# Attention values on 64 stationary columns in alternate column halves, with row sums made elementwise, in an fp32 language-model tower

## The reference, cut to what matters

```python
q = _l2norm(q) * q_scale
k = _l2norm(k) * k_scale
sim = jnp.einsum('bhid,bhjd->bhij', q, k) * SCALE
sim = sim + slopes * bias
sim = jnp.where(causal[None, None], -neg, sim)
attn = jax.nn.softmax(sim, axis=-1)
out = jnp.einsum('bhij,bhjd->bhid', attn, v)
return out.transpose(0, 2, 1, 3).reshape(b, n, h * dh) @ Wout
```

## Time and profile before

| | |
|---|---|
| median of 3 runs | 3293.55 us (3285.09 to 3293.67) |
| profiled execution | 3293.74 us, span from first to last instruction 3291.9 us |
| mean granted TensorE clock | 0.989 of full speed |
| busy: PE, PEld | 3111.8 us (95%), 1854.0 us (56%) |
| busy: DVE, ACT, POOL | 1701.1 us (52%), 1347.8 us (41%), 606.2 us (18%) |
| instructions | 42125 |

### The profile page before, as it was taken

How to read it: one execution, slowest core, us unless ns; L and a number is a source line. 1 busy time by engine, 2 the same in 40 slices (tenths; PEclk the granted TensorE clock), 3 DMA queues, 4 the chain that set the end, 5 groups by cost and what they waited for, 6 DMA issues and landing times.

```text
span 3291.9 us, 42125 instructions
## 1 busy us (share of the span) xinstructions
PE 3111.8 (95%) x14465; PEld 1854.0 (56%) x14465; DVE 1701.1 (52%) x4049; ACT 1347.8 (41%) x2588; POOL 606.2 (18%) x1020
## 2 busy tenths in 40 slices
PE   1699999999999998999999999999999999999999
PEld 1365656565555554656565656565555555666666
DVE  4555545454555557555554555454555553444444
ACT  2244544454545454545444545454545443111111
POOL 4430303030323031213030303030303000000000
PEclk9899999999999998999999999999999999999999
DMA  1000000000010000000000000000000100000000
GB/s 33 20 16 6 15 6 17 4 17 4 18 28 20 1 20 1 15 6 15 6 15 6 17 4 17 4 17 4 20 1 16 58 1 0 1 1 26 1 0 26
DMA packets 72100, 41.38 MB, mean 13 GB/s; under 512 B 14929, under 2 KB 70865, under 8 KB 71889
## 3 DMA queue, kind: packets, MB, share of 16 engines
q1 hardware_dynamic: 70352, 34.50, 4.0%
q0 software_dynamic: 1536, 4.20, 0.4%
HBM read 17.55 MB, written 4.19 MB: 7 GB/s over the span
## 4 chain that ended last, share of the span: by engine, by line
PE 89%; DVE 5%; issue 2%; ACT 2%; POOL 2%; DMA 0%; SPq 0%; DVEq 0%; ACTq 0%; POOLq 0%
PE ps L1034 29%; PE ps L994 8%; PE ps L1086 8%; PE ps L1072 7%; PE ps L1018 7%; PE ps L1044 7%; PE ps L1019 7%; PE ps L965 7%; PE ps L962 4%; PE ps L979 2%; PE ps L1022 1%; DVE h L820 1%; ACT arena L618 1%; DVE mx L794 1%; PE ps L996 1%
## 5 line engine op out<-in xcount | busy, mean ns | idle before, releaser
L636 ACT ACTIVATE probs<-ps,btab 128x512 f32<-128x512 f32 (+4 forms) x1408 | 831.3, 591 | 1143.9 <-PE ps L1019 628.6
L794 DVE TENSOR_REDUCE mx<-ps 128x1 f32<-128x512 f32 (+4 forms) x1408 | 794.4, 568 | 921.4 <-PE ps L994 504.0
L1034 PE MATMUL ps<-probs,arena 128*128 128x512 f32 (+4 forms) x2816 | 1234.1, 518 | 0.0
L1034 PEld LDWEIGHTS ps<-probs,arena 128*128 128x128 f32 (+1 forms) x2816 | 478.5, 190 | 125.9 <-ACT probs L636 18.1
L994 PE MATMUL ps<-arena 66*128 66x512 f16 (+4 forms) x1408 | 477.5, 341 | 19.9 <-DVE mx L794 8.8
L1018 PE MATMUL ps<-arena 128*128 128x512 f16 (+4 forms) x1408 | 467.8, 332 | 2.0 <-DMA arena<-augs 2.0
L1019 PE MATMUL ps<-arena 65*128 65x512 f16 (+4 forms) x1408 | 468.5, 333 | 0.0
L1044 PE MATMUL ps<-wo,otf 128*128 128x257 f32 x1024 | 316.0, 390 | 17.9 <-ACT arena L618 16.2
L965 PE MATMUL ps<-wqkv,xT 128*128 128x256 f32 (+1 forms) x1088 | 281.8, 382 | 0.0
L535 POOL TENSOR_TENSOR rnorm<-nsq,minus_half 128x4 f32<-128x4 f32 (+1 forms) x272 | 276.8, 1018 | 22.7 <-POOL nsq L532 0.2
L532 POOL TENSOR_SCALAR nsq<-ssq 128x4 f32<-128x4 f32 (+1 forms) x272 | 61.5, 226 | 1188.2 <-DVE ssq L760 1188.2
(11 more groups left out here) (121 smaller groups left out, 2625.2 us busy)
## 6 DMA issues: line engine op xcount, KB each, us to landing
arena<-arena SPq DMA_DIRECT2D x256, 64.0 KB, 2.1
wqkv<-in_Wkv SPq DMA_DIRECT2D x32, 128.0 KB, 2.4
arena<-in_w SPq DMA_DIRECT2D x2, 2048.0 KB, 11.3
out<-h SPq DMA_DIRECT2D x8, 512.0 KB, 2.9
wqkv<-in_Wq SPq DMA_DIRECT2D x16, 128.0 KB, 2.5
wo<-in_Wout SPq DMA_DIRECT2D x32, 64.0 KB, 2.2
h<-in_table,idx POOLq DMA_INDIRECT x32, 2.8
arena<-augs SPq DMA_DIRECT2D x32, 4.0 KB, 1.7
```

What stands on the lines that cost most here:

```text
L636: nc.scalar.activation(probs[0:rows, n % 4, 0:w], bank(S0 + n % 2)[0:rows, 0:w], ACT.Exp, bias=btab[0:rows, hh, z:z + 1]).then_inc(exp_don ...
L794: nc.vector.tensor_reduce(mx[:, it, c:c + 1], bank(k % 2)[:, 0:w], AX.X, ALU.max).then_inc(a_read, 1)
L1034: mm(bank(O0 + o % 2)[:, c0:GW], vt[t % 2][0:rows, jt, hd:hd + 2, :].rearrange("p a d -> p (a d)"), probs[0:rows, n % 4, 0:GW - c0], start ...
```

## The change

The stationary operand of L1034 becomes the 64 columns of values alone. In the groups ig = 1, 2 and 3 even key tiles go to array columns 0 to 63 (bank partitions 0 to 63) and odd ones to columns 64 to 127 (partitions 64 to 127); in group 0 all go to the first half. Two blocks, an even and the odd `m` behind it, are put at one time of the plan, so that their products follow each other. `probs` has 6 buffers.

The row sums: every block's exponentials are added to a tile `acc` (a copy for jt = 0), by POOL in groups 0 and 3 and by DVE in groups 1 and 2 (`sum_p`). At a group's end one product `sums` of 64 stationary columns of ones with `acc` gives the sums in a shared bank, which ACT copies (`keep_sums`). The two halves of a group's bank are joined: ACT copies the upper half to `otb` (`keep_o`), DVE adds the lower half to it (`join`) into `otf`. `wout` and `add_o` stay what they are, two units later. Some steps have times moved by 0.1 to 0.3 units, and the gate's small tiles move into the arena.

```diff
     def attend(t, t0):
         for m in range(PAIR):
             at(t0 + m, "scores", t, m)
             at(t0 + m + 0.5, "exp", t, m)
-            at(t0 + m + 2.4, "values", t, m)
+            at(t0 + m + 1.6, "sum_p", t, m)
+            at(t0 + (m | 1) + 2.4, "values", t, m)
         for hd in range(2):
             for ig in range(NG):
-                e0 = t0 + hd * BLKS + last_block[ig] + 3.7
-                at(e0, "keep_o", t, hd, ig)
+                e0 = t0 + hd * BLKS + last_block[ig] + 5.7
+                at(e0 - 1.5, "sums", t, hd, ig)
+                at(e0 - 1.0, "keep_o", t, hd, ig)
+                at(e0 - 1.0, "keep_sums", t, hd, ig)
+                at(e0 - 0.4, "join", t, hd, ig)
                 for k in range(G):
                     at(e0 + 0.8 + 1.6 * k, "wout", t, hd, ig, k)
-                    at(e0 + 1.5 + 1.6 * k, "add_o", t, hd, ig, k)
+                    at(e0 + 1.4 + 1.6 * k, "add_o", t, hd, ig, k)
...
+    def side(ig, jt):
+        return jt % 2 if ig else 0
...
+                if jt == 0:
+                    need(pool, l_ready, o - 1)
+                    pool.tensor_copy(a, probs[0:rows, n % PB, 0:GW - c0]).then_inc(sum_pool, 1)
+                else:
+                    pool.tensor_tensor(a, a, probs[0:rows, n % PB, 0:GW - c0], ALU.add).then_inc(sum_pool, 1)
...
             def exp(t, m):
-                need(act, pv_done, n - 3)
+                need(act, pv_done, n - PB + 1)
+                if n >= PB:
+                    on_pool, count = summed[n - PB]
+                    act.wait_ge(sum_pool if on_pool else sum_dve, count)
...
             def keep_o(t, hd, ig):
-                nc.scalar.activation(otf[:, o % 2, :], bank(O0 + o % 2), ACT.Copy).then_inc(o_read, 1)
+                if ig:
+                    need(act, joined, joins[o] - 1)
+                    nc.scalar.activation(otb[:, :], bank(O0 + o % 2)[DH:128, :], ACT.Copy).then_inc(o_read, 1)
+                else:
+                    nc.scalar.activation(otf[0:DH, o % 2, :], bank(O0 + o % 2)[0:DH, :], ACT.Copy).then_inc(o_read, 1)
...
+            def join(t, hd, ig):
+                    nc.vector.tensor_tensor(otf[0:DH, o % 2, :], bank(O0 + o % 2)[0:DH, :], otb[:, :], ALU.add).then_inc(joined, 1)
...
             def values(t, m):
-                mm(bank(O0 + o % 2)[:, c0:GW], vt[t % 2][0:rows, jt, hd:hd + 2, :].rearrange("p a d -> p (a d)"), probs[0:rows, n % 4, 0:GW - c0],
-                   start=(jt == 0), stop=(jt == G * ig + G)).then_inc(pv_done, 1)
+                z = side(ig, jt)
+                mm(bank(O0 + o % 2)[DH * z:DH * z + DH, c0:GW], vt[t % 2][0:rows, jt, hd, :], probs[0:rows, n % PB, 0:GW - c0],
+                   start=(jt == z), stop=(jt == G * ig + G - z)).then_inc(pv_done, 1)
+
+            def sums(t, hd, ig):
+                pe.wait_ge(sum_pool if on_pool else sum_dve, count)
+                z = shared_bank("sums", t, hd, ig)
+                mm(bank(z)[DH:128, :], ones[:, :], acc[:, o % 2, :], start=True, stop=True).then_inc(l_ready, 1)
```

More of the change, by code:

```diff
@@ L51, in lm_tower_kernel @@
     last_block = [max(m for m in range(BLKS) if blocks[m][0] == ig) for ig in range(NG)]
+    def side(ig, jt):
+        return jt % 2 if ig else 0
+    summed = {}
+    for n in range(PAIRS * 2 * BLKS):
+        on_pool = blocks[n % BLKS][0] in (0, NG - 1)
+        summed[n] = (on_pool, 1 + sum(1 for i in summed if i // (2 * BLKS) == n // (2 * BLKS) and summed[i][0] == on_pool)
+                     + sum(1 for m in range(2 * BLKS) if (blocks[m % BLKS][0] in (0, NG - 1)) == on_pool) * (n // (2 * BLKS)))
+    joins = {}
+    for o in range(PAIRS * 2 * NG):
+        joins[o] = sum(1 for i in range(o + 1) if i % NG)
+    PB = 6
     units = []
@@ L68, in at @@
     def at(time, kind, *which):
-        plan.append((time, len(plan), kind, which))
+        plan.append((round(time, 4), len(plan), kind, which))
     PAIR = 2 * BLKS
@@ L181, in lm_tower_kernel @@
     plan.sort()
-    SHARED = ("scores_a", "turn_shift", "wout", "turn", "turn_x", "turn_y", "logits", "null_turn")
+    SHARED = ("sums", "scores_a", "turn_shift", "wout", "turn", "turn_x", "turn_y", "logits", "null_turn")
     shared, nth = {}, {}
@@ L549, in q_rows_ @@
                     need(pool, rstd_ready[k], done[f"root{k + 1}"])
+                need(pool, sum_pool, done["sum_p"])
                 pool.tensor_copy(low[t % 2][ROW:ROW + 2, 0, hd, 0:N],
@@ L552, in q_rows_, with sum_p @@
                 pool.wait_ge(q_rows, 2 * t + hd + 1)
-            done = dict(inv_norm=0, scale_k=0, root1=0, root2=0, root3=0)
+            done = dict(inv_norm=0, scale_k=0, root1=0, root2=0, root3=0, sum_p=0)
+            def sum_p(t, m):
+                n = PAIR * t + m
+                ig, jt, rows, c0 = blocks[m % BLKS]
+                o = (2 * t + m // BLKS) * NG + ig
+                on_pool, count = summed[n]
+                if not on_pool:
+                    return
+                a = acc[0:rows, o % 2, c0:GW]
+                pool.wait_ge(exp_done, n + 1)
+                need(pool, sum_pool, count - 1)
+                if jt == 0:
[3 more added lines that the diff above has]
+                    pool.tensor_tensor(a, a, probs[0:rows, n % PB, 0:GW - c0], ALU.add).then_inc(sum_pool, 1)
             for _, _, kind, which in plan:
+                if kind == "sum_p":
+                    sum_p(*which)
                 if kind == "constants":
@@ L570, in _ @@
                     q_rows_(*which)
-                if kind in done:
+                if kind in done and (kind != "sum_p" or summed[PAIR * which[0] + which[1]][0]):
                     done[kind] += 1
@@ L890, in _ @@
                     add_o(*which)
+                elif kind == "sum_p":
+                    sum_p(*which)
+                elif kind == "join":
+                    join(*which)
                 elif kind == "ssq":
@@ L1096, in _ @@
                     scores_a(*which)
+                elif kind == "sums":
+                    sums(*which)
                 elif kind == "turn_shift":
```

87 lines of the change are left out of this document (60 added, 27 removed).

## The result

The changed kernel takes 3349.09 us (median of 4 runs, 3341.59 to 3356.33), the kernel before on the same chip 3292.64 us. The ratio is 1.0176, with an interval of 1.0142 to 1.021: slower, by less than half of the 4.3% forecast. The profiled execution's span is 3354.0 us, against 3291.9.

The account below looks back on a forecast made before the run. TensorE's order of work was taken to bound the kernel: overlap -193, switches +203, last tiles -24, row sums +110 and lateness +45 make +141 us on about 3294, giving 3435 us; range 3300 to 3640, own range 3360 to 3520.

Parts of the forecast that it names:

- TensorE's order of work sets the time: Whole kernel: each microsecond put on or taken off TensorE counts in full while DVE and POOL keep up.
- If TensorE starts passes in order, B1 can start beside A2 but not beside A1: Values products, two passes each (A1, A2, then B1, B2): one pass saved, -193 us, bounds 0 and -386.
- three sets of starts: Sign on PE, full pair: B1 starts at 0.43 us if forecast holds, 0.86 without overlap, near 0 with full overlap.
- The first rival: Values products: the two halves run beside each other throughout, saving twice 193 us, 3242 us in all; chance 0.16.
- The switches, +203: TensorE: 783 runs of narrow products pay for entering, leaving and exposed weight loads when the array's shape changes, +203 us.
- Last tiles, -24: Last tiles of groups: 128 blocks of 2 rows get cheaper inside runs already counted, -24 us.
- sums, +110: Row sums on TensorE: 128 products of two 512-column passes at 0.86 us each, +110 us.
- lateness, +45: In-order queues of other engines come late for TensorE: +45 us, estimated between 0 and 120.
- POOL as the bound: Rival: POOL's adds at 1.4 us fill group 3's stretch; at 1.83 they overrun it, 3560 us; chance 0.15.
- The feared path through POOL's inverse norms: Inverse norms queue behind POOL's adds, delaying DVE's unit and maxima, then PE's projections and first scores; 14 us wait before.
- The sums are late: Rival: PE reaches sums before the last add is done; needs 4 us lateness, folded into the 0 to 120.
- The forecast charged no wait: SBUF port sharing of DVE and POOL: no wait charged, as DVE's operation inside POOL's took 0.69 instead of 0.68 us.

Follow-up runs that it names:

- the first experiment: Changed kernel without any additions of exponentials on POOL and DVE (acc a constant 1, both products and copies kept): 3238.5 us, ratio 0.9849.
- the run without overlap: Changed kernel with both blocks of a pair put in the same column half, joins and sums kept: 3640.5 us (one run).
- the fourth experiment: Changed kernel with the second sequence's gathers at units 50 to 69.5 of pair 4, one wait for four: 3342.0 us, ratio 1.0162.

## Why the prediction was wrong, step by step

The direction was right and the time inside the whole range of 3300 to 3640 us, though just below the forecast's own 3360 to 3520. The size was not right, because two terms were off in opposite directions.

- **TensorE's order of work sets the time: right, with an end.** It holds while the others keep up, and they do less so in the new order: in the first experiment TensorE waits 124 us longer for DVE although DVE has none of the adds, and in the run without overlap 118 us longer although TensorE has more work than before. (DVE's shares in the earlier trace rows are 45 to 60%, not 55 to 61%.)
- **The failed step: "If TensorE starts passes in order, B1 can start beside A2 but not beside A1".** The -193 should have been -386, its lower bound. B1 starts 7 ns after A1 and ahead of A2, and four full passes take 1.01 us in the place of 1.86. Of the three sets of starts that were to tell the cases apart (B1 at 0.43, at 0.86, near 0), the trace shows the last. The passes of one fp32 product are not a block in a queue that other products stand behind; only those of the same half are. The first rival's mechanism held, with a chance of 0.16. Its argument from separate columns was the better one, and "all matmuls in the trace start in program order" was no evidence: the kernel before never had two halves. The Trainium skill has it in one sentence (TensorEngine Tiling (Array Packing), Key Properties: different tiles can execute in parallel); here it holds for fp32 products too. Another page of the Trainium skill says that matmuls start and end strictly in program order (TensorE: Matmul & The Clock Gate, Part 3); the records here order the passes A1, B1, A2, B2. In which order the passes reach the engine they don't show, so this row neither bears that rule out nor goes against it.
- **The switches, +203: right in the price of each.** 0.095 us to enter and 0.095 to leave, at 0.09 each in the forecast, and 0.05 for the first load. **Last tiles, -24, and sums, +110: not contradicted.** Sums with copies and switches gave 120.6 where the terms have 128. Together the three terms are 289 us, and TensorE's busy time rose by 255 in the run without overlap.
- **The second failed step: lateness, +45, bounded at 120.** The sum with full overlap is 3294 - 386 + 203 - 24 + 110 = 3197; the time is 3349, so 152 us are lateness. Even the upper bound was below it. About 110 are the adds' and 41 are there without them. Most of it is plain waiting: TensorE is idle for 136 us more than before. Of these the run without overlap, with all adds, joins and runs of two, already has 92, and the adds on the kernel before bring 21; the other 44 come with the overlap. What was missed, then: first the new order itself (two blocks' products in a row, joins, `sums`), for whose waits the forecast has no term of its own: without any adds the idle time is still 60 us above that of before. Which of its parts does it no run separates. Missed too: the adds cost 4.7 us a steady pair where the forecast took 2; the gathers in POOL's queue (12 us by the fourth experiment; no part of the forecast names them, though they are an old entry in a queue that the change filled); and the clock. By the page's mean, TensorE had (1 - 0.977) x 2 x 3354 = 154 us at the lower level, against 72 before; 82 us at half speed lose at most 41 us, chiefly in pair 6 and from pair 15 on. Whether the idle TensorE brings the low clock there or is prolonged by it was not separated.
- **The errors hide each other.** -193 and +107 give the -86 us between 3435 and 3349. With the first step right and the second as it was, the forecast would have been the rival's 3242, 107 too low and on the wrong side of the time before. The size of a gain on TensorE and the lateness of the others are one sum, not two: in the run without overlap, lateness by this sum is 3640 - 3583 = 57 us (3583 being the sum without the 45; by TensorE's idle time it is 92), with overlap 152.
- **POOL as the bound: not so.** Its add took 1.28 us, below the 1.4 of that rival. Timeline windows of the stretches from pair 3 (group 2 and group 3 of the first head, group 2 of the second) show it with room left:

```profile
688.70:719.20 30.50, 28.33 (x162) 15.87 (x160) 24.74 (x57) 16.03 (x33) 11.87 (x19) 1.00 0.05 12
719.20:750.20 31.00, 29.24 (x156) 12.88 (x154) 18.53 (x40) 18.58 (x37) 25.28 (x29) 1.00 0.13 35
...
773.60:793.40 19.80, 18.32 (x89) 7.22 (x88) 17.79 (x40) 8.81 (x15) 0.00 (x0) 1.00 0.00 0
```

The second row is POOL's fullest long stretch, 25.3 of 31.0 us (82%). DVE comes nearer: 24.7 of 30.5 in the first (81%) and 17.8 of 19.8 in the third (90%).
- **The feared path through POOL's inverse norms: nearly nothing.** DVE's wait for them went from 14.2 to 22.8 us in all. **The sums are late: in part so.** TensorE waits up to 33 us for the last adds, 2.4 at the longest; it is in the 152.
- **Busy times:** DVE 2086 (forecast near 2160), POOL 1291 (near 1200).

## What to carry to other kernels

A gain on the engine that bounds a kernel is paid out only down to the point where the next queue is late: 386 us less on TensorE gave 291. And the new order has a price of its own: with no gain at all TensorE stood idle for 92 us more. So price an edit with the lateness at the new pace and in the new order, and move work away from the queue whose results free the bounding engine's buffers (here DVE's maxima), even to an engine that takes twice as long for it. Before filling an idle engine, list what already stands in its queue with a wait: gathers that cost nothing beside an idle POOL cost 12 to 30 us beside a busy one.

## What the runs showed of the hardware

**Two fp32 products in the two column halves run side by side in full.** Four passes of 512 columns take 1.01 us in two halves and 1.86 in one, from the first's start to the next matmul, with the switches in both; eight passes in two halves take 1.87 (runs of four blocks).

**DVE's operations with two inputs in SBUF and POOL's adds shut each other out, for whole instructions.** The forecast charged no wait, since DVE's operation ran at full speed inside POOL's inverse norm. Beside POOL's adds it does not. Timeline of the kernel with all adds on POOL (L840 is L778 of before, L601 the add):

```profile
214.30 2.95 POOL L601 TENSOR_TENSOR acc<-acc,probs 128x512 f32<-128x512 f32 x2
214.60 1.51 DVE L840 TENSOR_TENSOR blk<-tqk,blk 128x512 f16<-128x512 f32 x1
```

By the single records, POOL's first add ends 0.96 us after DVE's operation began, and that operation ends 0.55 us later; POOL's second add begins meanwhile, takes 1.54 us instead of 1.27, and ends 1.13 us after DVE's. By group, in the same kernel and in the one with no adds:

```profile
L840 DVE TENSOR_TENSOR blk<-tqk,blk 128x512 f16<-128x512 f32 x128 | 118.1, 923 | 14.8 <-ACT blk L655 14.8
```

```profile
L827 DVE TENSOR_TENSOR blk<-tqk,blk 128x512 f16<-128x512 f32 x128 | 87.5, 684 | 14.6 <-ACT blk L644 14.6
```

923 against 684 ns over 128 of them is 31 us of DVE. This is the exclusive lock of the Trainium skill (SBUF — State Buffer, section "SBUF: two separate sides"), and the trace agrees where POOL's operation reads 512 columns of two tiles (a cast of 2 partitions by 2048 columns in the changed kernel held up one of DVE's adds too: 1.43 us in the place of 0.68); beside one that reads 4 columns it shows nothing. By the single records of the changed kernel, 15 of the 128 operations begin inside one of POOL's adds: each takes 1.36 to 1.48 us and ends 0.55 us after that add; 53 begin inside an inverse norm and take 0.68 to 0.69 like the other 60. That is 10 us in all, so for these operations the lock is a small part of the 152 us.

**The clock.** What the lower level costs can be read twice. Pairs 8 and 9 of the changed kernel have 3.4 us at 1.2 GHz each and take 1.4 to 1.5 us more than the undisturbed ones. And over the twelve executions of the kernel with all adds on POOL and four gathers a pair, the time goes from 3269.5 us at a mean clock of 0.986 to 3289.5 at 0.976, by a straight line through all twelve 2.1 us for each 0.001; by that, an estimate, the step from 0.989 before to 0.977 in the changed kernel is about 25 of the 152 us. How long TensorE is idle in all does not give the clock: no adds 240 us and 0.988, all adds on POOL 281 and 0.977, the changed kernel 316 and 0.977, alternate adds 364 and 0.984, runs of four 384 and 0.968. What brings the lower level more in one kernel than in another stays open.
